# Shorter expert choice at the end of VectorE's step, second norm on ScalarE, scatters in groups of four

## The reference, cut to what matters

```
x = x + tanh(g0) * (attention(layernorm(x), context) @ Wu.T + bu)     # q and k normalised per head
n = layernorm(x)
probs = softmax(n @ Wg)                      # 8 experts
vals, idx = top_k(probs, 2)
weights = vals / (sum(vals) + 1e-9)
routed = sum over the two of weights * (silu(n @ W1[e] + b1[e]) @ W2[e] + b2[e])
shared = silu(n @ Ws1 + bs1) @ Ws2 + bs2
x = x + tanh(g1) * (routed + 0.1 * shared)
```

## Time and profile before

| | |
|---|---|
| median of 3 runs | 715.66 us (713.71 to 716.74) |
| profiled execution | 712.84 us, span 710.8 us |
| busy in the span | PE 585.2, PEld 519.6, DVE 490.7, ACT 453.8, POOL 362.4 us |
| mean granted TensorE clock | 0.943 |

### The profile page before, as it was taken

One profiled execution on the slowest core, in us unless ns is written; L12 is line 12 of the kernel. 1 busy time (PEld: TensorE's weight loads), 2 busy tenths in 40 slices (PEclk: granted clock), 3 DMA queues, 4 the chain that ended last, 5 costly groups with the idle time before them and its releaser, 6 DMA issues.

```text
span 710.8 us, 21126 instructions
## 1 busy us (share of the span) xinstructions
PE 585.2 (82%) x7614; PEld 519.6 (73%) x7614; DVE 490.7 (69%) x1045; ACT 453.8 (64%) x982; POOL 362.4 (51%) x706
## 2 busy tenths in 40 slices
PE   3889999999789799889789877753889898989850
PEld 1678888888578677678677666643879898989850
DVE  5688898989889889889989874534324444444427
ACT  4588889998688688778778654430425454545425
POOL 3455555655446456667766653657002444545540
PEclk9799999999999999999999999977899999999985
DMA  6800101001001001001000000113201222222218
GB/s 240 256 2 3 32 18 32 18 2 47 3 17 32 17 11 54 8 17 56 9 18 10 10 16 17 39 37 136 61 0 39 69 69 69 73 67 77 70 63 326
DMA packets 22582, 38.01 MB, mean 53 GB/s; under 512 B 5232, under 2 KB 13040, under 8 KB 22352
## 3 DMA queue, kind: packets, MB, share of 16 engines
q1 hardware_dynamic: 17648, 27.27, 12.0%
q0 software_dynamic: 4544, 9.38, 3.7%
q10 hardware_dynamic: 288, 0.00, 0.0%
HBM read 23.17 MB, written 13.47 MB: 52 GB/s over the span
## 4 chain that ended last, share of the span: by engine, by line
PE 57%; DVE 22%; issue 8%; another core or an unknown queue 4%; ACT 4%; DMA 3%; POOL 1%; SPq 0%; ACTq 0%; DVEq 0%; POOLq 0%
PE ps L1333 8%; PE ps L1111 5%; PE ps L1137 5%; PE ps L1079 4%; PE ps L1120 4%; PE ps L1081 4%; PE ps L1080 4%; PE ps L1167 4%; PE ps L1319 3%; DVE sm L767 3%; PE ps L1321 3%; PE ps L1235 3%; DVE wide L745 3%; PE ps L1152 3%
## 5 line engine op out<-in xcount | busy, mean ns | idle before, releaser
L661 POOL DMA_INDIRECT results<-spo,xs_ix x78 | 75.4, 966 | 116.9 <-DVE spo L1053 102.0
L398 ACT ACTIVATE qk_T<-ps,lnw 128x512 f32<-128x512 f32 x128 | 96.7, 787 | 45.3 <-PE ps L1111 44.8
L517 ACT ACTIVATE qk_T<-ps,b_cols 128x256 f32<-128x256 f32 x156 | 61.9, 475 | 77.1 <-PE ps L1321 74.2
L1111 PE MATMUL ps<-ident,wide 128*128 128x128 f32 x512 | 80.3, 283 | 35.6 <-DVE x_res L721 34.2
L1111 PEld LDWEIGHTS ps<-ident,wide 128*128 128x128 f32 x512 | 60.3, 148 | 53.5 <-DVE x_res L721 42.2
L1079 PE MATMUL ps<-w_hi,xc_hi 128*128 128x512 f32 x192 | 89.9, 468 | 8.1 <-DVE wide L745 3.9
L745 DVE TENSOR_TENSOR wide<-ps,rstd 128x512 f32<-128x512 f32 x128 | 87.1, 681 | 4.4 <-POOL rstd L607 4.4
L738 DVE TENSOR_REDUCE ss<-wide 128x16 f32<-128x1024 f32 x64 | 77.6, 1212 | 11.1 <-ACT wide L374 10.8
L1081 PE MATMUL ps<-w_hi,xc_lo 128*128 128x512 f32 x192 | 78.9, 411 | 0.0
L374 ACT ACTIVATE wide<-ps 128x512 f32<-128x512 f32 x128 | 76.0, 595 | 3.6 <-PE ps L1081 3.5
L1080 PE MATMUL ps<-w_lo,xc_hi 128*128 128x512 f32 x192 | 78.1, 407 | 0.0
(11 more groups left out here) (171 smaller groups left out, 1387.3 us busy)
## 6 DMA issues: line engine op xcount, KB each, us to landing
v_sb<-routed SPq DMA_DIRECT2D x39, 130.0 KB
xc_in<-in_x SPq DMA_DIRECT2D x8, 256.0 KB, 3.0
xc_in<-in_ctx SPq DMA_DIRECT2D x8, 256.0 KB, 4.6
w_raw<-in_L_ffn_W SPq DMA_DIRECT2D x8, 256.0 KB, 2.6
wide<-results SPq DMA_DIRECT2D x4, 512.0 KB, 5.0
rows_all<-results SPq DMA_DIRECT2D x4, 512.0 KB, 8.3
out_x<-x_res SPq DMA_DIRECT2D x8, 256.0 KB, 4.2
x_res<-in_x SPq DMA_DIRECT2D x1, 1792.0 KB, 8.7
```

The lines of the kernel that those rows point to most:

```text
L398: nc.scalar.activation(qk_T[:, n, 4 * j:4 * j + 4, :].rearrange("p a n -> p (a n)"), ps[6 + j][:, :], ACT.Identity, bias=lnw[:, 2 * n + 1: ...
L661: gp_.indirect_dma_start(out=results[:, :], out_offset=bass.IndirectOffsetOnAxis(ap=xs_ix[:, b4, a:a + 1], axis=0), in_=yb[:, b4, a, :], i ...
L1111: last = nc.tensor.transpose(ps[6 + j][:, a * P:(a + 1) * P], qk_n[:, n, c0:c0 + P], ident[:, :])
```

## The change

- `normalise` moves from VectorE to ScalarE, behind `values(1, s)`: one ACTIVATE Identity with scale `rstd_2` and bias `shift_2`. POOL makes `shift_2` = -mean x rstd in a third small instruction of `second_rstd`.
- `route` moves from behind `row_inverses` to the end of VectorE's step, and begins one step earlier (ROUTE_LAG 11).
- The choice is made on logits less their highest instead of on probabilities. Softmax's division, `fill_ranks` and `count`'s reduce go; ScalarE makes a second small exponential (`second_exponentials`, of `f_top`). A batch takes 22 VectorE instructions in place of 34.
- TensorE's `ranks` makes all ranks in PSUM: nine bf16 matmuls of 72 down to 8 columns in place of two of 8 columns.
- The scatters start three steps earlier (SCATTER_LAG 17), so 13 tiles are left behind the loop, and these go by two tiles, four scatters, each group g from the second on waiting for `h_done` of 4 g, which is `shared_hidden(g - 1)`.
- The schedule has one more small instruction (`sched[:, 3]`), for the number that names a row's first expert.

```diff
-        SCATTER_LAG = 20
+        SCATTER_LAG = 17
+        ROUTE_LAG = 11
...
+            def normalise(t):
+                if has(t):
+                    sc.wait_ge(rstd2_ready, t + 1)
+                    nc.scalar.activation(rows_all[:, t, 0:D], x_res[:, t, :], ACT.Identity, bias=shift_2[:, t:t + 1],
+                                         scale=rstd_2[:, t:t + 1]).then_inc(norm_ready, 1)
...
+            def second_exponentials(b):
+                sc.wait_ge(f_top, b + 1)
+                nc.scalar.activation(e1, top, ACT.Exp).then_inc(f_e1, 1)
...
+                    nc.gpsimd.tensor_scalar(shift_2[:, t:t + 1], mv_2[:, t, 0:1], rstd_2[:, t:t + 1], -1.0, ALU.mult, ALU.mult).then_inc(rstd2_ready, 1)
...
-            for t in range(LAST_STEP - SCATTER_LAG + 1, TILES):
+            rest = range(LAST_STEP - SCATTER_LAG + 1, TILES)
+            for i, t in enumerate(rest):
+                g, odd = divmod(i, 2)
+                if odd == 0 and g >= 1:
+                    gp_.wait_ge(h_done, CH * min(g, GROUPS))
                 scatter(t)
...
+                ve.wait_ge(f_sub, b + 1)
+                after(nc.vector.scalar_tensor_tensor(tie, gp, 0.0, first_of, ALU.is_equal, ALU.mult))
+
+            def first_choice(b):
+                first = rows_all[:, BT * b:BT * b + BT, D + 1]
+                after(nc.vector.tensor_reduce(first, tie, AX.X, ALU.max))
+                after(nc.vector.tensor_tensor(oh[:, 0, :, :], tie, by_expert(first), ALU.is_equal))
+                after(nc.vector.scalar_tensor_tensor(rest, oh[:, 0, :, :], -3.0e38, gp, ALU.mult, ALU.add))
+
+            def highest_of_rest(b):
+                nc.vector.tensor_reduce(top, rest, AX.X, ALU.max).then_inc(f_top, 1)
+                ve.wait_ge(f_top, b + 1)
+                after(nc.vector.tensor_tensor(tie, rest, by_expert(top), ALU.is_equal))
+                after(nc.vector.tensor_tensor(tie, tie, first_of, ALU.mult))
+
+            def second_choice(b):
+                after(nc.vector.tensor_reduce(lead, tie, AX.X, ALU.max))
+                after(nc.vector.tensor_tensor(oh[:, 1, :, :], tie, by_expert(lead), ALU.is_equal))
+                nc.vector.tensor_tensor(picked[:, 0:BT, :], oh[:, 0, :, :], oh[:, 1, :, :], ALU.add).then_inc(f_cnt, 1)
...
                 if at == 0:
                     less_highest(b)
                 if at == 1:
+                    first_choice(b)
                 if at == 2:
+                    highest_of_rest(b)
                 if at == 3:
+                    second_choice(b)
+                if at == RANKS_AT:
+                    place(b)
                 if at == 5:
+                    denominators(b)
                 if at == 6:
                     weigh(b)
...
             def step(s):
                 row_sums(s - 1)
                 row_inverses(s - 1)
-                route(s, 12)
...
                 scale(0, 1, s + 1)
-                normalise(s - 3)
                 token_statistics(s + 3)
...
-                route_ranks(s, 12)
+                route_ranks(s, ROUTE_LAG)
                 keep_logits(s - 4)
+                route(s, ROUTE_LAG)
...
             def ranks(b):
                 pe.wait_ge(f_cnt, b + 1)
+                flat = picked[:, :, :].rearrange("p j e -> p (j e)")
+                nc.tensor.matmul(ps[5][:, E:E + (BT + 1) * E], before[:, :], flat, start=True, stop=False)
+                for k in range(1, BT + 1):
+                    last = nc.tensor.matmul(ps[5][:, E + k * E:E + (BT + 1) * E], ones_b[:, :], flat[:, 0:(BT + 1 - k) * E],
+                                            start=False, stop=(k == BT))
+                last.then_inc(f_rank, 1)
```

More of the change, by code:

```diff
@@ L459, in route @@
                     expert_exponentials(b)
+                if b is not None and at == 2:
+                    second_exponentials(b)
             def hi_part(g):
@@ L815, in ties @@
[L815 to L837, removed]
@@ new lines, in take_ranks, with place @@
+            def take_ranks(b):
+                ve.wait_ge(f_rank, b + 1)
+                nc.vector.tensor_tensor(rank, ps[5][:, E:E + BT * E].rearrange("p (j e) -> p j e", j=BT),
+                                        base[:, b, :].unsqueeze(1).to_broadcast([P, BT, E]), ALU.add).then_inc(f_taken, 1)
+                nc.vector.tensor_tensor(base[:, b + 1, :], ps[5][:, E + BT * E:2 * E + BT * E], base[:, b, :], ALU.add).then_inc(f_taken, 1)
+            def place(b):
+                ve.wait_ge(f_taken, 2 * b + 2)
+                after(nc.vector.tensor_tensor(hit, oh, rank.unsqueeze(1).to_broadcast([P, 2, BT, E]), ALU.mult))
+                with nc.allow_low_precision("slots are whole numbers"):
+                    nc.vector.tensor_reduce(slot[:, b, :, :], hit, AX.X, ALU.add).then_inc(f_slot, 1)
@@ L842, in weigh, with denominators @@
+            def denominators(b):
+                ve.wait_ge(f_exp, b + 1)
+                after(nc.vector.tensor_reduce(gs, ge, AX.X, ALU.add))
+                after(nc.vector.tensor_scalar(den, gs, TOPK_EPS, 1.0, ALU.mult, ALU.add))
+                ve.wait_ge(f_e1, b + 1)
+                after(nc.vector.tensor_tensor(den, den, e1, ALU.add))
             def weigh(b):
                 tiles = slice(BT * b, BT * b + BT)
-                after(nc.vector.tensor_scalar(gs, top[:, 0, :], TOPK_EPS, None, ALU.add))
@@ L845, in weigh @@
[L845 to L853, removed]
@@ L855, in place @@
-            def place(b):
-                ve.wait_ge(f_taken, 2 * b + 2)
-                after(nc.vector.tensor_tensor(rank, fill[0][:, pad_rows:, :], mine.unsqueeze(1).to_broadcast([P, BT, E]), ALU.add))
-                after(nc.vector.tensor_tensor(hit, oh, rank.unsqueeze(1).to_broadcast([P, 2, BT, E]), ALU.mult))
-                after(nc.vector.tensor_reduce(slotf, hit, AX.X, ALU.add))
-                nc.vector.tensor_copy(slot[:, b, :, :], slotf).then_inc(f_slot, 1)
+                after(nc.vector.reciprocal(den, den))
@@ L862, in route @@
+                after(nc.vector.tensor_scalar(wtok[:, tiles, 0], den, tg[:, 1:2], None, ALU.mult))
+                after(nc.vector.tensor_tensor(wtok[:, tiles, 1], wtok[:, tiles, 0], e1, ALU.mult))
             def route(s, lag):
@@ L905, in clear_fill @@
                 ve.wait_ge(wv_ready, 2)
-                for a in fill:
-                    nc.vector.memset(a, 0.0).then_inc(run0, 1)
-                ve.wait_ge(run0, 2)
+                nc.vector.memset(picked[:, BT, :], 0.0).then_inc(run0, 1)
+                ve.wait_ge(run0, 1)
                 ve.wait_ge(gp_const, 6)
@@ L963, in _ @@
             lo_part(2)
-            expert_probabilities(NB - 1)
-            highest(0, gp)
-            ties(0, gp)
-            chosen(0)
-            without_first()
-            highest(1, rest)
-            ties(1, rest)
-            chosen(1)
-            count(NB - 1)
-            fill_ranks(NB - 1)
-            name_first(NB - 1)
+            first_choice(NB - 1)
+            highest_of_rest(NB - 1)
+            second_choice(NB - 1)
+            denominators(NB - 1)
             weigh(NB - 1)
@@ L1194, in ranks @@
                 pe.wait_ge(f_cnt, b + 1)
-                nc.tensor.matmul(ps[5][:, E:2 * E], before[:, :], cnt_b[:, b, :], start=True, stop=True)
-                nc.tensor.matmul(ps[5][:, 2 * E:3 * E], ones_b[:, :], cnt_b[:, b, :], start=True, stop=True).then_inc(f_rank, 1)
+                flat = picked[:, :, :].rearrange("p j e -> p (j e)")
[4 more added lines that the diff above has]
+                last.then_inc(f_rank, 1)
             def route_ranks(s, lag):
```

74 lines of the change are left out of this document (24 added, 50 removed).

## The result

The changed kernel took 676.29 us (median of 4 runs, 675.32 to 677.05), the kernel before 714.68 us: a ratio of 0.947, 95% interval 0.942 to 0.953. Forecast were 669 us, with 650 to 688 as the range, so 7 us are missing. The profiled execution went from 712.84 to 677.05 us, its span from 710.8 to 675.3.

The account below looks back on a forecast made before the run. TensorE bounds the kernel, held up in the loop by VectorE's choice and behind it by scatters delaying its updates. Profiled 712.84 - 31 (choice) + 3 (norm) - 19 (tail) + 0.2 = 666, median 669 us, range 650 to 688.

Parts of the forecast that it names:

- The moved choice: Loop after the first routing: 22 steps at 11.15 us take 245.3, freeing 47.5; new place costs 16.4; 31 us back.
- collisions: Loop, new place: two-input slice instructions stopped beside POOL's L581 or L570; 4 us charged, bounds 0 to 12.
- The scatters in the loop: Loop steps given scatters by the shorter lag: no cost charged, since step 24 held two and took 11.13 us.
- The norm: Loop: nothing gained on VectorE; ScalarE's added instruction of 0.39 us charged at 0.1 us a step, 3 us in all.
- The tail: Behind the loop, up to the routed tiles: 5.4 us back at the first stop, 14.0 at the second, together 19.
- The first series of 12: Behind the loop: twelve scatters without a pause, 448.4 to 463.6 us, TensorE's updates coming through at 465.9.
- the first stop: Behind the loop: ScalarE's wait during the first scatter series, to end near 19 us behind the loop's last residual.
- Result 1: Shared expert behind the loop: it would end at some 470.5 us in place of 475.9, 5.4 us back.
- ScalarE's second stop: Behind the loop: the wait during the second scatter series goes, with 11.91 us of TensorE idle; 14.0 us back.
- the groups still hold: Rival for the tail: TensorE's updates late behind each group of four, 4 us back, not 19; 684 us, chance 0.14.
- The sum: Whole kernel: 712.84 (profiled) - 31 + 3 - 19 + 0.2 = 666 us; median 2.8 above that, say 669.
- The sign of being wrong: Loop and tail: the prediction is wrong if steps stay over 12.5 us or a gate is followed by a TensorE stop.

Follow-up runs that it names:

- its four variants: Changed kernel with the choice at its old place (661.97 us), the norm on VectorE (632.47), no waits between scatter groups (634.69), or both scatters moved within the step (645.65).
- the parted variant: Changed kernel with a step's two scatters parted on GpSimd, the second issued behind the second norm's rstd; 659.15 us, against 677.43 for the changed kernel.

## Why the prediction was right, and where it was off

**The moved choice**: right in its mechanism. It was to give 31 us, 28 with the norm. Without the stretched scores the loop gives 292.8 - 254.1 = 39 us, norm included (two chips of one kind). The forecast put 16.4 + 3 = 19.4 us on top of 245.3; what is left is 254.1 - 245.3 = 8.8. Of L581 and L570, whose collisions were charged with 4 us, L570 does not collide (L583 in the changed kernel):

```profile
161.24 0.23 DVE L815 TENSOR_TENSOR w_raw<-lg_all,w_raw 128x64 f32<-128x64 f32 x1
161.34 0.57 POOL L583 TENSOR_TENSOR rstd<-ve,expo 128x1 f32<-128x1 f32 x1
161.50 0.23 DVE L817 SCALAR_TENSOR_TENSOR w_raw<-w_raw,first_e 128x64 f32<-128x64 f32 x1
```

A slice beside the one-column power (L583) runs at its full pitch. L581 (L596 now) is another matter: the slices fell so that reductions ran beside it and two-input instructions overlapped only its last 0.02 us. Whether it would stop one is not shown, and that no 4 us were lost to it may be luck. The rule of the Trainium skill (SBUF — State Buffer, Who interferes with whom), by which the collisions would have cost 12 us, agrees with the two-input instruction stopped at the old place and not with these rows.

**The scatters in the loop**: the step that failed. "The scatters moved into the loop meet a step that held two already: step 24 had them and took 11.13" charged nothing. That step was a poor witness: the burst of scores right behind its end, the residual of 326.54, is the only one of before that was stretched, and the 11.13 us do not contain it. Measured is 17.0 us for 16 bursts, about 1.1 us each. The shorter lag put scatters into three more steps (16 in place of 13), but in the kernel before one burst was stretched and not 13: most of the price comes from TensorE arriving 2 to 3 us earlier, measured against the second scatter. What the moved choice won let TensorE run into it.

**The norm**: forecast 3 us, measured 0 to 2. Its instruction was sized at 0.39 us from one (L535) with a scale from memory; this one has scale and bias from memory and takes 0.50.

**The tail**: 14.2 us in place of 19. The first series of 12 came as counted, and the first stop ended 19.6 us behind the last residual, as forecast. Result 1 ended 25.7 us behind that residual, where 24.2 were forecast. Two terms were off. ScalarE's second stop (19.36 us) did not go but became two of 6.88 and 5.36 us: the late slots let 10 scatters through at once, and even a group of 4 holds an update back until about 1 us behind it. TensorE's 11.91 us of idle time did go, as forecast. But that TensorE itself would stand with nothing but "issue" in front of it (gaps of up to 1.65 us during the first two series) was not foreseen. The stretch took 71.5 us where 66 were forecast. As the rival "the groups still hold" had it, groups do hold, but by 5 us and not by 15: groups alone were worth 18.7 us on the kernel before and 8.7 on the changed one.

**The sum** (666 us forecast for the profiled execution, 677 measured): -39 for choice and norm, +17 for the scores, -14 behind the loop, together -36; measured -35.8 profiled. Two errors of the loop, 11 us too little gain and 17 too little cost, cancelled in part. So it is partly luck that 669 came so near: on a chip of this kind the changed kernel with the stretched bursts taken out, the parted variant, takes 659 us. And the profiled execution came out 11 us above its forecast, the median only 7 above: it was put 2.8 us above the profiled execution and stands 0.8 below it.

Of the signs named, residuals of 11.5 to 12 us failed in the steps with scatters (12.6), the residual's wait under 12 us (5.7), no slice beside the multiply, and TensorE over 93% busy (252.76 of 271.59, 93.1%) held, the last with stretched matmuls in it; in the tail the first stop ended at 19.6 us as named, while "none over 3 us" behind it failed. The sign of being wrong, steps that stay over 12.5 us, came true from step 17 on (12.5 to 12.8), though not for the reason that it was meant for: the choice no longer held them up.

**Open**: what makes two chips differ, and how a scatter delays TensorE's updates and matmuls. No run looks inside that. No run shows either where the 42 us between the chips lie for the kernel before, which was not traced on the faster one. The changed kernel itself was not run there; its time is only argued from its variants (634.7 us without groups, 632.5 with the norm on VectorE). Nor was the long choice run at the new place, so what shortening it gave by itself is not measured.

## What to carry to other kernels

When a stall goes, redraw what every other engine issues at the time at which the freed one will now arrive: a transfer that was harmless for being early can land on the burst behind it. Put scatters one at a time into waits that their engine has anyway, and pause them against work that TensorE can do while its updates are late. Before trusting a small gain, see whether the chip is one on which the stall occurs at all.

## What the runs showed of the hardware

- The same kernel took 634.7 us on one chip and 686.0 on another. On three of the four chips ScalarE takes up what TensorE has finished only 1 to 3 us behind the last of a series of indirect scatters, which GpSimd issues at a pitch of 1.26 us (read here as TensorE's semaphore updates arriving late); on the fourth ScalarE never stood for more than 4.4 us in a series of 28, and TensorE's own work ended that.
- In the three, 64 matmuls of 64x64 take 2.0 to 2.5 us in place of 1.16 when the second of two scatters runs beside them; with only the first ahead, overlapping by 0.1 us, 1.16. 16 matmuls of 128x128 beside a scatter take 1.95 us and 1.96 without.
- The routed part, too, differs: from the first routed tile to the end 178 to 183 us for the changed kernel on the chips with late updates, 167 for its four variants on the chip without. Why was not looked into.
- A small two-input VectorE instruction that begins beside GpSimd's 128x1024 multiply is stopped until that ends (0.23 us become 1.81), and not at all by its 128x1 power of 0.57 us. A one-input TENSOR_SCALAR of 128x8 is stopped by the multiply as well (0.17 us become 1.48, in the variant with the old place), while reductions run through beside it in 0.21 us.
